# A recommendation model on one core: embeddings as TensorE's stationary operand in layer 1, W1's low part and the norms' statistics read from PSUM, the last sums as column products

## What is computed

```python
E = jnp.concatenate([emb_cat, emb_cont], axis=1)          # 2048 x 39 x 64
s = jnp.sum(E, axis=1)
fm_second = 0.5 * jnp.sum(s * s - jnp.sum(E * E, axis=1), axis=1)
deep = E.reshape(E.shape[0], -1)                           # 2048 x 2496
h = jax.nn.relu(_batchnorm(deep @ W1 + b1, g1, be1))       # 1024 channels
h = jax.nn.relu(_batchnorm(h @ W2 + b2, g2, be2))          # 512 channels
deep_out = (h @ W3 + b3)[:, 0]
out_pos = jax.nn.sigmoid(bias + fm_first + fm_second + deep_out)[:, None]
return jnp.concatenate([1.0 - out_pos, out_pos], axis=1)
```

## Time and profile before

| | |
|---|---|
| median of 3 runs | 884.25 us (884.24 to 885.12) |
| profiled execution, span | 645.4 us |
| TensorE busy | 522.1 us (81%) |
| GpSimd busy | 399.0 us (62%) |
| VectorE busy | 216.2 us (33%) |
| ScalarE busy | 191.7 us (30%) |
| read from HBM | 26.56 MB |
| mean granted TensorE clock | 0.904 |

### The profile page before, as it was taken

How to read it: one execution, slowest core, us unless ns; L and a number is a source line. 1 busy time by engine, 2 the same in 40 slices (tenths; PEclk the granted TensorE clock), 3 DMA queues, 4 the chain that set the end, 5 groups by cost and what they waited for, 6 DMA issues and landing times.

```text
span 645.4 us, 9108 instructions
## 1 busy us (share of the span) xinstructions
PE 522.1 (81%) x3324; PEld 467.0 (72%) x3324; DVE 216.2 (33%) x428; ACT 191.7 (30%) x405; POOL 399.0 (62%) x423
## 2 busy tenths in 40 slices
PE   0839999969766977698679966997698778999993
PEld 0139989968766877687577956796688777788882
DVE  1362252214221422142205220522052235654366
ACT  1351231212111211121113110321031225897655
POOL 5787777777777777777777777777777760000000
PEclk9958997997999798979987999788979878999996
DMA  8963234323332333234323432333234520000000
GB/s 284 296 133 28 29 28 28 27 26 27 27 28 25 28 27 26 27 28 27 27 27 26 27 28 27 26 28 26 27 27 60 123 25 0 2 1 1 1 0 1
DMA packets 18021, 26.74 MB, mean 41 GB/s; under 512 B 7602, under 2 KB 7834, under 8 KB 18010
## 3 DMA queue, kind: packets, MB, share of 16 engines
q0 software_dynamic: 13312, 13.87, 27.5%
q1 hardware_dynamic: 4384, 12.66, 5.5%
q10 hardware_dynamic: 314, 0.07, 0.1%
HBM read 26.56 MB, written 0.02 MB: 41 GB/s over the span
## 4 chain that ended last, share of the span: by engine, by line
POOL 54%; issue 19%; PE 16%; DMA 4%; DVE 3%; ACT 3%; POOLq 0%; SPq 0%; DVEq 0%; ACTq 0%
POOL emb L249 54%; PE bank L696 10%; DMA h<-in_w 4%; PE bank L631 2%; PE bank L658 2%; ACT h L388 1%; PE bank L681 1%; DMA emb<-in_table,idx_now 1%; DVE h L612 0%; DVE stats L557 0%; ACT hhi L351 0%; PE bank L731 0%; DVE stats L490 0%; DVE mv L544 0%; DVE zpart L592 0%
## 5 line engine op out<-in xcount | busy, mean ns | idle before, releaser
L249 POOL DMA_INDIRECT emb<-in_table,idx_now x416 | 398.2, 957 | 130.7 <-issue 130.7
L658 PE MATMUL bank<-xhi,w1hi 128*128 128x256 f32 x832 | 254.6, 306 | 0.0
L658 PE MATMUL bank<-xlo,w1hi 128*128 128x256 f32 x832 | 245.4, 295 | 0.0
L658 PE MATMUL bank<-xhi,w1lo 128*128 128x256 f32 x832 | 244.9, 294 | 0.0
L658 PEld LDWEIGHTS bank<-xhi,w1hi 128*128 128x128 f32 x832 | 170.0, 204 | 0.0
L658 PEld LDWEIGHTS bank<-xlo,w1hi 128*128 128x128 f32 x832 | 170.0, 204 | 0.0
L658 PEld LDWEIGHTS bank<-xhi,w1lo 128*128 128x128 f32 x832 | 169.1, 203 | 0.0
L442 DVE TENSOR_TENSOR xlo<-bank,xhi 128x256 fp32r<-128x256 f32 x104 | 44.0, 423 | 351.6 <-ACT xhi L282 351.6
L282 ACT ACTIVATE xhi<-bank 128x256 fp32r<-128x256 f32 x104 | 39.8, 383 | 377.4 <-PE bank L646 377.4
L646 PE MATMUL bank<-ident,emb 128*128 128x128 f32 x208 | 45.6, 303 | 76.7 <-DMA emb<-in_table,idx_now 74.8
L646 PEld LDWEIGHTS bank<-ident,emb 128*128 128x128 f32 x208 | 23.7, 146 | 93.0 <-DMA emb<-in_table,idx_now 85.3
...
## 6 DMA issues: line engine op xcount, KB each, us to landing
...
emb<-in_table,idx_now POOLq DMA_INDIRECT x416, 3.3
...
diag<-in_cont_diag ACTq DMA_DIRECT2D x1, 45.5 KB, 3.0
```

Source lines behind the costliest of these rows:

```text
L249: nc.gpsimd.indirect_dma_start(out=emb[:, j, at:at + ROW], out_offset=None, in_=table, in_offset=bass.IndirectOffsetOnAxis(ap=idx_now[:, j ...
L658: done = nc.tensor.matmul(acc[c], w[:, k, cols], x[:, s, :], start=False, stop=(last and n == 2), skip_group_check=True)
```

## The change

1. Blocks 0 to 6: x (128 columns of `xhi` or `xlo`) is the stationary operand and 512 channels of W1 move: 12 matmuls for a k-tile, sums with batch rows on the partitions. ScalarE copies the four banks into the columns of `h1` that belong to the last block (`stage`), TensorE transposes them back into the banks (`turn`), ScalarE evicts them (`sums_out`, one instruction for a bank). b1 comes in as a 14th row of `m_sb` against a row of ones in `cont_sb`. The first transposes and the small products of the next block are put ahead of `turn`. The squares of the continuous features are made at the end of the block before.
2. Last block: the old form, without the loop. From k-tile 8 on, products of tile k-1 stand ahead of the transposes of tile k. The last tile's products with `xhi` stand ahead of those with `xlo` (`multiply_last`), and each bank is signalled by itself.
3. W1: ScalarE makes `w1hi`, then copies the tile in two halves to PSUM banks 2 and 3; VectorE subtracts `w1hi` (SBUF) from the bank. The copies to `m_sb` follow k-tile 8 instead of 3.
4. Statistics of the last block of layer 1 and of all of layer 2 are read from PSUM ahead of the eviction; b2 is added to the mean in `norm`. Layer 1's norm is in five parts, and the orders of ScalarE and VectorE between the layers are written out anew.
5. The end: the last weighted sum of chunk 2 stands behind the statistics of chunk 3; the last relu reads PSUM with the bias folded in; the sums over channels are products with one moving column (`z_part`: 128 columns of `h1` stationary, a column of ones or of W3 moving) into PSUM, which replace transposes and reductions. 13 matmuls (`WARM_PRODUCTS`) whose result is not used stand between them.

The diff, cut to its core (ScalarE, then VectorE, then TensorE):

```diff
             for k in range(KT):
                 act.wait_ge(raw_in[k], 16)
                 nc.scalar.activation(w1hi[:, k, :], raw[:, raw_slot(k), :], ACT.Copy).then_inc(w1hi_ready, 1)
-                if k == 3:
+                for half in range(2):
+                    if k:
+                        act.wait_ge(w1_free[half], k)
+                    nc.scalar.activation(w1_bank[half][:, :], raw[:, raw_slot(k), half * 512:(half + 1) * 512],
+                                         ACT.Copy).then_inc(w1_full[half], 1)
+                if k == RAW_SLOTS - CONT_KT - 1:
                     act.wait_ge(m_done, 1)
                     for half in range(2):
-                        nc.scalar.activation(m_sb[:, half * 512:(half + 1) * 512], bank[half][0:CONT, :],
+                        nc.scalar.activation(m_sb[0:CONT, half * 512:(half + 1) * 512], bank[half][0:CONT, :],
...
+            def stage(b, i):
+                half, j = sums[i]
+                act.wait_ge(sums_full, b * ACC_BANKS + (i + 1 + EMPTY))
+                chunks = h1[:, :, :].rearrange("p (q j) n -> p q j n", j=BT)[:, half * BT:(half + 1) * BT, j, :]
+                nc.scalar.activation(chunks[:, :, (BLOCKS - 1) * BC:],
+                                     bank[i][:, :].rearrange("p (q n) -> p q n", n=BC),
+                                     ACT.Copy).then_inc(staged, 1)
             def sums_out(b, m):
                 act.wait_ge(acc_full, b * ACC_BANKS + (m + 1 + EMPTY))
-                for c in (2 * m, 2 * m + 1):
-                    done = nc.scalar.activation(h1[:, c, ds(b * BC, BC)], acc[c], ACT.Identity,
-                                                bias=b1[:, c:c + 1])
-                done.then_inc(acc_free[m], 1)
+                nc.scalar.activation(h1[:, 2 * m:2 * m + 2, ds(b * BC, BC)],
+                                     bank[m][:, :].rearrange("p (c n) -> p c n", n=BC),
+                                     ACT.Copy).then_inc(acc_free[m], 1)
...
+            def last_sums_out(m):
+                act.wait_ge(stats1_done, C1 * (BLOCKS - 1) + 2 * m + 2)
+                sums_out(BLOCKS - 1, m)
...
+                cont_squares(b + 1)
+                for i in range(ACC_BANKS):
+                    stage(b, i)
                 for m in range(ACC_BANKS):
                     sums_out(b, m)
...
+            std1(0)
             act.wait_ge(norm1_ready, 1)
-            for k in range(early):
-                hidden(0, k)
-            sums_out(b, 2)
-            sums_out(b, 3)
-            std(bn1, mv1, *NORM_PARTS[1], mean1_ready, std1_ready)
+            hidden_high(0, 0)
+            std1(1)
+            hidden_full(0, 0)
             act.wait_ge(norm1_ready, 2)
-            for k in range(early, C1):
-                hidden(0, k)
+            hidden_high(0, 1)
+            hidden_full(0, 1)
+            std1(2)
+            last_sums_out(0)
+            act.wait_ge(norm1_ready, 3)
+            hidden_high(0, 2)
+            hidden_full(0, 2)
+            last_sums_out(1)
+            std1(3)
+            hidden_high(0, 3)
...
+            last_sums_out(2)
+            hidden_high(0, 5)
+            hidden_full(0, 5)
+            last_sums_out(3)
+            act.wait_ge(norm1_ready, 5)
+            for k in range(6, C1):
+                hidden_high(0, k)
...
+                act.wait_ge(stats2_done, n * C2 + m + 1)
...
+            def out2(m, n):
+                act.wait_ge(acc2_free, (N2 - 1) * C2 + (m + 1 if n == N2 - 1 else 0))
+                x = h1[:, m, n * NB2:(n + 1) * NB2]
+                nc.scalar.activation(x, x, ACT.Relu, bias=bn2[:, SHIFT, m:m + 1],
+                                     scale=bn2[:, SCALE, m:m + 1]).then_inc(out2_ready, 1)
+            for m in range(C2 - 1):
+                std(bn2, mv2, m, m + 1, mean2_ready, std2_ready)
                 sums2_out(N2 - 1, m)
-                std(bn2, mv2, m, m + 1, mean2_ready, std2_ready)
                 act.wait_ge(norm2_ready, m + 1)
                 for n in range(N2):
-                    x = h1[:, m, n * NB2:(n + 1) * NB2]
-                    nc.scalar.activation(x, x, ACT.Relu, bias=bn2[:, SHIFT, m:m + 1],
-                                         scale=bn2[:, SCALE, m:m + 1]).then_inc(out2_ready, 1)
+                    out2(m, n)
+            m = C2 - 1
+            std(bn2, mv2, m, m + 1, mean2_ready, std2_ready)
+            act.wait_ge(norm2_ready, m + 1)
+            for n in range(N2 - 1):
+                out2(m, n)
+            act.wait_ge(shift_ready, 1)
+            nc.scalar.activation(h1[:, m, (N2 - 1) * NB2:], bank2(N2 - 1, m), ACT.Relu, bias=out_shift[:, :],
+                                 scale=bn2[:, SCALE, m:m + 1]).then_inc(out2_ready, 1)
...
-                nc.vector.tensor_tensor(w1lo[:, k, :], raw[:, raw_slot(k), :], w1hi[:, k, :].bitcast(f32),
-                                        ALU.subtract).then_inc(w1_ready, 1)
+                for half in range(2):
+                    cols = slice(half * 512, (half + 1) * 512)
+                    dve.wait_ge(w1_full[half], k + 1)
+                    nc.vector.tensor_tensor(w1lo[:, k, cols], w1_bank[half][:, :], w1hi[:, k, cols].bitcast(f32),
+                                            ALU.subtract).then_inc(w1_free[half], 1)
...
+                if bias is None:
+                    chained(nc.vector.tensor_tensor(bn[:, MEAN_SCALE, lo:hi], mv[:, lo:hi, 0],
+                                                    bn[:, SCALE, lo:hi], ALU.mult))
+                else:
+                    chained(nc.vector.scalar_tensor_tensor(
+                        out=bn[:, MEAN_SCALE, lo:hi], in0=mv[:, lo:hi, 0], scalar=bias[:, lo:hi],
+                        in1=bn[:, SCALE, lo:hi], op0=ALU.add, op1=ALU.mult))
...
+            def last_stats(c):
+                dve.wait_ge(acc_full, b * ACC_BANKS + (c // 2 + 1 + EMPTY))
+                nc.vector.bn_stats(stats1[:, c, b, :], acc[c]).then_inc(stats1_done, 1)
+            def mean1(c):
+                dve.wait_ge(stats1_done, C1 * b + c + 1)
+                nc.vector.bn_aggr(mv1[:, c, :],
+                                  stats1[:, c, :, :].rearrange("p b s -> p (b s)")).then_inc(mean1_ready, 1)
...
+                dve.wait_ge(acc2_full, n * C2 + m + 1)
+                nc.vector.bn_stats(stats2[:, m, n, :], bank2(n, m)).then_inc(stats2_done, 1)
+            last_stats(0)
+            mean1(0)
+            last_stats(1)
             norm1(0)
-            stats(b, 1)
-            for k in range(early):
+            mean1(1)
+            last_stats(2)
+            last_stats(3)
+            norm1(1)
+            mean1(2)
+            mean1(3)
+            h_low(0, 0)
+            h_low(0, 1)
+            norm1(2)
+            last_stats(4)
+            last_stats(5)
+            mean1(4)
+            mean1(5)
+            h_low(0, 2)
+            last_stats(6)
+            last_stats(7)
+            mean1(6)
+            mean1(7)
+            norm1(3)
+            h_low(0, 3)
+            norm1(4)
...
+            for m in range(C2):
+                statistics2(N2 - 1, m)
+                mean2(m)
+                if m == C2 - 1:
+                    weighted(m - 1, N2 - 1)
+                norm(bn2, mv2, b2, g2, be2, m, m + 1, std2_ready, m, norm2_ready)
+                if m < C2 - 1:
+                    for n in range(N2 - (m == C2 - 2)):
+                        weighted(m, n)
+            dve.wait_ge(norm2_ready, C2)
+            scale, shift = bn2[:, SCALE, m:m + 1], bn2[:, SHIFT, m:m + 1]
+            nc.vector.scalar_tensor_tensor(out=out_shift[:, :], in0=scale, scalar=b2[:, m:m + 1], in1=shift,
+                                           op0=ALU.mult, op1=ALU.add).then_inc(shift_ready, 1)
+            for n in range(1, N2):
+                weighted(m, n)
+            dve.wait_ge(z_done, 1)
+            nc.vector.tensor_tensor(zsum[:, :], z, fm[:, :], ALU.add).then_inc(z_ready, 1)
...
+            def tile_products(k, i, stop=False):
+                half, j = sums[i]
+                cols, channels = slice(j * P, (j + 1) * P), slice(half * HALF, (half + 1) * HALF)
+                for n, (w, x) in enumerate(((w1hi, xhi), (w1lo, xhi), (w1hi, xlo))):
+                    done = nc.tensor.matmul(bank[i][:, :], x[:, k % XT, cols], w[:, k, channels], start=False,
+                                            stop=stop and n == 2, skip_group_check=True)
+                return done
+            def x_wait(b, k):
+                pe.wait_ge(split_done[k % TP], TP_USES[k % TP] * b + (k // TP + 1 + EMPTY))
+                for half in range(2):
+                    pe.wait_ge(w1_free[half], k + 1)
+            def multiply_tiles(b, k):
+                x_wait(b, k)
+                for i in range(ACC_BANKS):
+                    done = tile_products(k, i, k == KT - 1)
+                    if k == KT - 1:
+                        done.then_inc(sums_full, 1)
+                if k < KT - 1:
+                    done.then_inc(x_used[k % XT], 1)
```

(83 more changed lines are left out.)

181 lines of the change are left out of this document (92 added, 89 removed).

## The result

| | median us | runs |
|---|---|---|
| before | 884.53 | 884.24 to 885.12, 4 |
| changed | 899.61 | 897.24 to 903.34, 4 |

The ratio is 1.0183 (95% interval 1.0147 to 1.0219): 15 us slower, where 12.3 us faster was forecast. I call the first kind of chip prompt and the second late, for a reason that the rows give.

The account below looks back on a forecast made before the run. Layer 1 was taken as bound by GpSimd's issue of gathers, 65 us a block. Gains of 4.47 + 3.4 + 0.3 + 4.1 = 12.3 us gave a span of 633.1 and a time of 872.0 us, range 869.8 to 877.0.

Parts of the forecast that it names:

- the time around the span moves: Sign that the forecast is wrong: the 238.9 us between profiled span and median time, taken as unchanged, changes.
- the stall: Layer 2's matmuls, 2.5 us lost before: one half-clock stretch (1.7 us) stays; gain 0.3 us, bounds +2 and -1.4.
- part 4: Layer 2's last product to the span's end: 10.05 us against 14.22, gain 4.1 us (3.5 to 4.5).
- Part 1: Embeddings stationary in the first 7 blocks: 5 us more a block, caught up at about tile 8; cost 0.
- Part 2: W1's low part from PSUM: gathers between 18.4 and 44.0 us no longer slow; gain 4.47 us, bounds 0 and 4.47.
- Part 3: Handover to layer 2: it starts 4.75 to 5.1 us behind the last transposes, before 8.37; gain 3.4 us (3.2 to 3.7).
- T: Point in time: the last pair of transposes in layer 1, from which the start of layer 2 is counted.
- E: Point in time: the end of layer 2's last product, from which the span's end is counted.
- A: Rival: the slow gathers stay slow, through transfers or because the subtraction still takes a port; 876.5 us, chance 0.13.
- B: Rival: TensorE idles more in the last block and begins layer 2 at half clock; 875.7 us, chance 0.10.
- D: Rival, no change: block 0's late start exceeds its slack by as much as the rest gains; 884 us, chance 0.03.
- C: Rival: at block boundaries TensorE's work exceeds the gathers' 65 us, so gathers wait in 7 blocks; 907 us, chance 0.06.

Follow-up runs that it names:

- experiment 6: Changed kernel with layer 1's blocks as before and four more fillers, on a late chip: 881.33 us beside 882.98 for the kernel before, ratio 0.9983.
- experiment 1: Kernel before, unchanged: 648.09 us; kernel before with only W1's low part taken from PSUM: 643.07 us, ratio 0.9927.
- experiment 2: Changed kernel, unchanged: 635.22 us beside 648.33 for the kernel before; with layer 1's blocks as before: 633.66; with 0 instead of 13 fillers: 636.39.
- experiments 2, 3 and 5: Changed kernel, unchanged, on three prompt chips: 635.22, 634.51 and 634.91 us; with layer 1's blocks as before: 633.66, 634.00 and 633.80.
- Experiment 4: TensorE's signals to ScalarE in the first 7 blocks delayed by two or three copies: kernel before 1019.06 and 1131.44 us, changed kernel 993.01 and 1126.72.

## Why the prediction was wrong, point by point

**The premise.** "The median of the runs shown is 884.25 us, so 238.9 us lie around the span. I take that part as unchanged" is the step that failed. Of the executions here that have both a time and a span, none has more than 2.9 us around it, and nearly all have 1.7 to 1.9. The profile of 645.4 us and the times of 884 come from two conditions, and in the second the span is 883.4 us (experiment 6), GpSimd idles 333.3 us of it ahead of gathers, and TensorE's late signals set the pace, not the issue of gathers. The prediction named "the time around the span moves" among what would make it wrong, and gave it no chance in the range. A ratio of 1.37 between a time and its span should have had a rival of its own.

**Its sum, where its premise holds.** On three prompt chips the change is worth 13.1, 13.4 and 14.0 us; 12.3 was forecast, and 645.4 + 1.7 - 12.3 = 634.8 for a measured 635.2. That it fits so well is partly luck: the stall and part 4 were together put at 4.4 us and brought 4.2, but one was too small by 1.9 and the other too large by 2.1. Term by term, on the spans of experiments 1 and 2:

- Part 1, cost 0: right on prompt chips within 1.6 us (experiments 2, 3 and 5). Its working was too dark: from block 2 on TensorE waits for rows from tile 4 or 5 on, not from tile 8. On late chips it is the loss.
- Part 2, 4.47: the last gather is 4.4 us earlier (alone it brought 5.4 to 6.7 us of time, above the forecast's upper bound of 4.47), no gather over 1.0 us in the window. The Trainium skill's rule ("SBUF — State Buffer", Who interferes with whom), by which this would bring 0, is contradicted by experiment 1: with one input moved to PSUM and the transfers about as they were, the gathers went from 1.21 us to 0.94. What fails is its inference that descriptors need only the write side. Its statement that such an operation contends with what GpSimd reads fits these gathers, whose row numbers lie in SBUF (`idx_now`); no run here parts the two.
- Part 3, 3.4: T to layer 2 is 4.84 us, within the forecast 4.75 to 5.1. Net of a last tile that comes 0.4 us later behind its gather it is 3.1.
- The stall in layer 2, 0.3: mis-sized. It is 2.2, above the bound of +2: with a pause of under 1 us ahead of it, layer 2 loses no stretch to the half clock, where I had kept one.
- Part 4, 4.1: mis-sized, 2.0 (span's end 12.2 behind E instead of 10.05; 11.2 to 12.5 in the four traces of the changed kernel). The 12 column products behind the weighted sums stand in the trace as 24 passes and take 4.37 us. A group of four takes 0.88 us at full clock and 1.7 at half, the sums come 0.71 apart, so they queue up and TensorE ends the chain 3.09 us behind VectorE (row at 631.50), where 0.85 was taken from transposes. The passes come 0.11 us apart at full clock and 0.21 at half, and the clock fell at 628.1, behind the first group.

**Rivals.** A fell (no slow gathers). B's half clock came at the other end, in the column products, for 1 us. D did not occur. C, given 0.06, is the nearest: gathers do wait for TensorE in each block. But its condition was wrong: a block does not need more than 65 us of TensorE's work; TensorE is held up by the gathers themselves.

**What the loss on late chips consists of** (changed minus before, 18.2 us of span; each of the two traces is the slowest execution of its kernel, and the medians are 15.1 apart): +3.4 to the first run of 20; +16.6 in six blocks; +3.4 from there to layer 2; -2.2 in layer 2; -3.0 behind it.

The six blocks, 2.8 us each: before, GpSimd pauses three times in a block, 14.20 + 7.01 + 9.22 = 30.4 us. In the changed kernel two of its groups run on into one of 32 gathers and it pauses twice, 18.61 + 14.53 = 33.1. Undoing part 1 brings the three pauses back (13.39 + 6.99 + 10.45 = 30.8). That part 1 does it is shown, within one reservation: the changed kernel's late trace and the other two are from different occasions, tied by the kernel before at 884.5 and 883.0. How it does it is in part argued: in the long run of gathers the signal of 487.64 is kept until 512.45, 36 us behind the run's first gather, and another signal in such a run takes 31.1 us, while of the signals given in a run of 16 none is kept for more than 15.5 us. Experiment 4 bears it out within one trace: its blocks with a run of 32 are 5 to 11 us longer than those without. Why part 1 lets two groups run on into one was not looked into.

Part 3's order: from tile 8 of the last block on, a tile's transposes are issued behind the products of the tile before, so that each tile waits for its own xhi and xlo. Where gathers set the pace (experiment 2) that wait lies inside the wait for rows, of which 0.91 us is left at the last tile. On a late chip all rows are there at 754, TensorE is the bound, and from tile 7 on it takes 22.9 us for five tiles (775.07 to 798.01) instead of 15.3 (755.68 to 771.00). Ahead of the products of four of them TensorE idles 0.93 us, as here:

```profile
782.29 0.39 PE L791 MATMUL bank<-xhi,w1hi 128*128 128x256 f32 x1 [0.93 <-DVE xlo L516]
```

One tile's products (2.9) of that are moved from behind T to ahead of it, the rest, 4.7, is new. From tile 7 to layer 2 it is 27.7 us against 23.6: 4.1 slower where 3.4 faster was forecast. This is read from the traces; no run undoes that order alone.

**Still open.** What makes a chip late, and whether it is the chip (none was met twice). How a program could be made proof against it was not tried. Without a delay put in, no kernel here beats the kernel before on a late chip by more than the 1.7 us of experiment 6, and the changed kernel was never measured on the same late chip as its version without part 1; on prompt chips the changed kernel without part 1 is the best, by about 1 us.
